# A four-layer-pair f32 transformer block on one core: narrow TensorE products gathered or widened, latent matrices folded, more weight and gate tiles, a new order table

## The reference, cut to what matters

```
x = x + L0_xattn(ctx, ctx, ln(x))      # one head, no mask
x = x + L0_ffn(ln(x))                  # switch-head: 8 heads x 8 experts, 2 chosen, values and output
x = x + L1_xattn(ln(x), ctx, ctx)      # 16 heads of 8, causal, lengths
x = x + L1_ffn(ln(x))                  # ternary weights, gelu, norm, 512 wide
x = x + L2_xattn(ln(x), ctx)           # 2 heads of 64, q and k normalized per head, mask
x = x + L2_ffn(ln(x))                  # 8 experts of 256, 2 chosen, with biases b1 and b2
x = x + L3_xattn(ln(x), ctx, ctx)      # 16 heads of 64, a bias on the scores
x = x + L3_ffn(ln(x))                  # see below
```

```
lat    = xf @ fc1.T                          # 128 -> 64
he[e]  = relu2(lat @ w1[e].T) @ w2[e].T      # 8 experts, 64 -> 64 -> 64, relu2(t) = max(t, 0)^2
comb   = sum over the 2 chosen experts of gate[e] * he[e]
routed = comb @ fc2.T                        # 64 -> 128
shared = relu2(xf @ up.T) @ down.T           # 128 -> 512 -> 128
out    = routed + shared
```

## Time and profile before

| what | value |
|---|---|
| runs | 685.36, 688.69, 686.41 us; median 686.41 us |
| span of the profiled execution | 682.8 us (the page gives no other time of its own) |
| PE busy | 654.7 us, 96% of the span |
| DVE, ACT, POOL busy | 523.3 us (77%), 372.4 us (55%), 203.6 us (30%) |
| mean granted PE clock | 9 tenths or more in all 40 slices but one |
| moved by DMA | 113.86 MB |

### The profile page before, as it was taken

One profiled execution on the slowest core, in us unless ns is written; L12 is line 12 of the kernel. 1 busy time (PEld: TensorE's weight loads), 2 busy tenths in 40 slices (PEclk: granted clock), 3 DMA queues, 4 the chain that ended last, 5 costly groups with the idle time before them and its releaser, 6 DMA issues.

```text
span 682.8 us, 14844 instructions
## 1 busy us (share of the span) xinstructions
PE 654.7 (96%) x5566; PEld 589.5 (86%) x5566; DVE 523.3 (77%) x1433; ACT 372.4 (55%) x1261; POOL 203.6 (30%) x244
## 2 busy tenths in 40 slices
PE   6889999999999999999999999999999998899898
PEld 5779999788989999998799998987899997669776
DVE  1987587995788889895788999887588866657756
ACT  2251421356664866236655686377647653966683
POOL 0010002832331422304424242135232532533140
PEclk9999999999999999999999999999999999899999
DMA  8979969987312916885346027577026500000000
GB/s 319 395 237 306 401 233 314 330 291 244 129 62 69 329 33 219 271 298 204 102 150 228 2 66 221 188 234 234 33 55 232 201 16 5 1 1 1 1 1 13
DMA packets 37655, 113.86 MB, mean 167 GB/s; under 512 B 9040, under 2 KB 11728, under 8 KB 37200
## 3 DMA queue, kind: packets, MB, share of 16 engines
q1 hardware_dynamic: 37584, 112.92, 47.9%
HBM read 111.86 MB, written 1.05 MB: 165 GB/s over the span
## 4 chain that ended last, share of the span: by engine, by line
PE 78%; DVE 12%; ACT 6%; DMA 2%; issue 1%; POOL 1%; DVEq 0%
PE bank L462 35%; PE e_bank L462 31%; PE p_bank L462 5%; PE bank L713 3%; ACT wide_b L1136 3%; DVE gated L1442 2%; DVE wide_b L1445 1%; DMA gated<-gates_of 1%; POOL wide_b L1346 1%; DVE max_neg L1728 1%; PE bank L702 1%; DVE f_route L1442 1%; ACT f_b L1045 1%; PE p_bank L562 1%; ACT wide_a L995 1%
## 5 line engine op out<-in xcount | busy, mean ns | idle before, releaser
L462 PE MATMUL e_bank<-weights,gated 128*128 128x128 f32 x2048 | 246.9, 277 | 0.3 <-ACT f_v L995 0.2
L462 PEld LDWEIGHTS e_bank<-weights,gated 128*128 128x128 f32 x2048 | 236.6, 192 | 8.2 <-issue 4.0
L1346 POOL TENSOR_TENSOR wide_b<-wide_b,row_inv 128x480 f32<-128x480 f32 x64 | 76.0, 1196 | 132.5 <-DVE row_inv L1733 132.4
L1136 ACT ACTIVATE wide_b<-wide_b,max_neg 128x120 f32<-128x120 f32 x272 | 103.5, 386 | 19.0 <-DVE max_neg L1728 16.3
L995 ACT ACTIVATE wide_a<-bank 120x512 f32<-120x512 f32 (+4 forms) x110 | 59.0, 545 | 50.9 <-PE bank L713 23.3
L1442 DVE TENSOR_TENSOR gated<-gated,f_xnT 128x1024 f32<-128x1024 f32 x64 | 81.9, 1302 | 6.3 <-DMA gated<-gates_of 5.8
L1442 DVE TENSOR_TENSOR gated<-gated,f_v 128x1024 f32<-128x1024 f32 x64 | 78.8, 1250 | 8.5 <-ACT f_v L995 4.2
L1338 POOL TENSOR_TENSOR rstd<-var_eps,w_const 128x1 f32<-128x1 f32 (+1 forms) x48 | 34.4, 717 | 144.6 <-DVE var_eps L1438 144.5
L1136 ACT ACTIVATION_READ_ACCUMULATOR wide_b<-wide_b,max_neg 128x1 f32 x272 | 52.3, 192 | 0.0
L713 PE MATMUL bank<-w_const,wide_b 128*120 128x128 f32 x256 | 40.4, 284 | 3.8 <-POOL wide_b L1346 3.7
L1728 DVE TENSOR_REDUCE max_neg<-wide_b 128x4 f32<-128x480 f32 x64 | 41.8, 653 | 2.2
(11 more groups left out here) (265 smaller groups left out, 1229.7 us busy)
## 6 DMA issues: line engine op xcount, KB each, us to landing
gated<-gates_of SPq DMA_DIRECT2D x128, 512.0 KB, 5.8
weights<-in_experts SPq DMA_DIRECT2D x64, 512.0 KB, 6.4
w_L2f<-in_L2f SPq DMA_DIRECT2D x1, 2124.0 KB, 14.6
w_L3x<-in_L3x SPq DMA_DIRECT2D x1, 2108.0 KB, 18.6
wide_b<-in_raw0f SPq DMA_DIRECT2D x1, 1024.0 KB, 7.9
w_L3f<-in_L3f SPq DMA_DIRECT2D x1, 1000.0 KB, 21.1
w_L1f<-in_L1f SPq DMA_DIRECT2D x1, 516.0 KB, 10.9
x_next<-in_x SPq DMA_DIRECT2D x4, 128.0 KB, 6.4
```

Source lines behind the costliest of these rows:

```text
L462: return nc.tensor.matmul(o, lhsT, rhs, start=first, stop=last)
L1136: last = nc.scalar.activation(p, p, ACT.Exp, bias=max_neg[lane][:, h:h + 1], accum_out=row_sum[lane][:, h:h + 1])
L1346: nc.gpsimd.tensor_tensor(p3, p3, row_inv[lane][:, 4 * i:4 * i + 4].unsqueeze(2).broadcast_to([128, 4, K]), ALU.mult).then_inc(probs_norme ...
```

## The change

1. `W_SLOTS` 4 to 6 and `G_SLOTS` 6 to 7. Four weight tiles stay where they were in the first loads; two more are loaded after the last weight pack, with a semaphore of their own.
2. The fourth L1 score product contracts all 128 rows: POOL makes a second block tensor in which all rows but the last 32 are zero.
3. The L1 mix and the L3 mix are one visit of 16 products each, after all four transposes. The L1 mix uses four groups of columns in turn.
4. The L2X scores are one product of K=128 and 240 columns; ACT makes the two heads' keys as two copies, each scaled by a column that is zero in the other head's rows. PE's wait for layer 3's keys moves behind the scores.
5. L2F: the gate sits in 128 columns, zero beyond the first 8; its transpose and the b2 product are whole.
6. L3F: at setup fc1 is multiplied into w1 and fc2 into w2, so the routed part is 128 -> 512 -> 128 like the shared one. DVE spreads the gate over 512 columns, PE transposes that in four pieces, DVE multiplies the squared hidden values by it, and four products add onto the shared sum in the same bank. w2's pack doubles from 256 to 512 columns.
7. The residual's identity product is gone; DVE adds `x_now` where it copied.
8. The table `ORDER` is new for all five engines. Its strings are not shown; of the first one a line:

```diff
-W_SLOTS, G_SLOTS = 4, 6
+W_SLOTS, EARLY_SLOTS, G_SLOTS = 6, 4, 7
...
-    "PE": "pppp0p0pp00pp0pppp0pp00pp0pppp0pffpffpfpfffpfffpf0pffffpfpfpfpfpffffpfffffpffffpfffpp0p101p0pfffpf1f0f"
...
+    "PE": "pppppp0000ppp0ppppp0000pppppppffpffpfffpfpffffpffffpfpfpfpfpffpfffffpffffpffpfffpp00p01p0ff1ffp01p0f"
...
     # SP, first loads
-                    for j in range(W_SLOTS):
-                        sp.dma_start(weights[j][:, :], experts[:, E * D * j:E * D * (j + 1)]).then_inc(first_experts, 16)
+                    first_weights(range(EARLY_SLOTS), first_experts)
...
+                    first_weights(range(EARLY_SLOTS, W_SLOTS), next_experts)
...
     # PE, front
-                                mm(e_bank[:, 0:2 * D], ident, f_x[pair % 2][:, :], True, False)
...
     # PE, setup
-                    mm(bank[1][0][:, 64:128], centre, part["L3f", "fc1"]).then_inc(centre_products, 1)
+                    mm(bank[1][0][0:64, 128:256], part["L3f", "fc1"], centre).then_inc(centre_products, 1)
+                    yield
+                    pe.wait_ge(centred, GATE_FC1)
+                    mm(bank[0][1][:, :], centred_fc1[0:64, :], part["L3f", "w1"][0:64, :]).then_inc(centre_products, 1)
+                    for p in range(4):
+                        last = mm(bank[1][1][:, 128 * p:128 * p + 128], part["L3f", "w2"][0:64, 128 * p:128 * p + 128],
+                                  part["L3f", "fc2"][0:64, :])
+                    last.then_inc(centre_products, 1)
...
     # PE, L1 scores and mix
-                    mm(bank[lane][0][:, 0:4 * K], small[lane][96:128, 0:S], wide_a[lane][96:128, 0:4 * K])\
+                    pe.wait_ge(blocks_ready[lane], blocks_ready.upto(L1X, 2, pair))
+                    mm(bank[lane][0][:, 0:4 * K], small[lane][:, 0:S], wide_a[lane][:, 512:512 + 4 * K])\
...
+                    for i in range(4):
+                        transpose_probs(L1X, i, lane)
+                        yield
+                    pe.wait_ge(blocks_ready[lane], blocks_ready.upto(L1X, 3, pair))
+                    pe.wait_ge(pT_ready[lane], pT_ready.upto(L1X, 4, pair))
+                    for c in range(4):
+                        for j in range(4):
+                            h = 4 * j + c
+                            last = mm(bank[lane][2][32 * j:32 * j + 32, 0:S], v[lane][0:K, 32 * h:32 * h + 32],
+                                      wide_a[lane][0:K, 128 * h:128 * h + 128], c == 0, c == 3)
+                    last.then_inc(mix_psum[lane], 1)
...
     # PE, L2X scores
-                    for h in range(H2X):
-                        r = slice(64 * h, 64 * h + 64)
-                        last = mm(bank[lane][2 * h][:, 0:K], wide_a[lane][r, 0:S], wide_a[lane][r, 1408:1408 + K])
-                    last.then_inc(scores_psum[lane], 1)
+                    mm(bank[lane][0][:, 0:2 * K], wide_a[lane][:, 0:S], wide_a[lane][:, 1408:1408 + 2 * K])\
+                        .then_inc(scores_psum[lane], 1)
...
     # PE, L2F
-                    mm(bank[lane][0][:, 0:D], gateT[lane][0:E, :], part["L2f", "b2"][0:E, :])\
+                    mm(bank[lane][0][:, 0:D], gateT[lane][:, :], part["L2f", "b2"])\
...
     # PE, L3F
+                    for to, name in ((0, "up"), (1, "w1")):
+                        for c in range(4):
+                            last = mm(bank[lane][to][:, 128 * c:128 * c + 128],
+                                      part["L3f", name][:, 128 * c:128 * c + 128], xnT[lane][:, :])
+                        last.then_inc(hidden_psum[lane], 1)
+                        yield
...
+                    pe.wait_ge(spread_ready[lane], spread_ready.upto(L3F, 1, pair))
                     for p in range(4):
...
+                        last = nc.tensor.transpose(bank[lane][2][:, 128 * p:128 * p + 128],
+                                                   spread[lane][:, 128 * p:128 * p + 128], ident)
+                    last.then_inc(turned_psum[lane], 1)
+                    yield
+                    pe.wait_ge(routed_gated[lane], routed_gated.upto(L3F, 1, pair))
                     for p in range(4):
...
+                        last = mm(bank[lane][0][:, 0:D], wide_a[lane][:, 512 + 128 * p:640 + 128 * p],
+                                  part["L3f", "w2"][:, 128 * p:128 * p + 128], False, p == 3)
+                    last.then_inc(out_psum[lane], 1)
...
     # DVE, L3F
-                    for odd in range(2):
-                        last = tt(wide_b[lane][:, 1024 + 256 * odd:1280 + 256 * odd].rearrange("p (c u) -> p c u", u=64),
...
-                    nc.vector.tensor_reduce(comb[lane],
...
+                    ts(spread[lane].rearrange("p (e i) -> p e i", i=64), r[6].unsqueeze(2).broadcast_to([128, E, 64]),
+                       one[2], None, ALU.mult).then_inc(spread_ready[lane], 1)
+                    yield
...
+                    tt(wide_a[lane][:, 512:1024], wide_a[lane][:, 512:1024], bank[lane][2][:, :], ALU.mult)\
+                        .then_inc(routed_gated[lane], 1)
```

More of the change, by code:

```diff
@@ L247, in build @@
         q2_turned = below[:, 0:D]
+        centred_fc1 = below[:, D:2 * D]
         p_products = Course("p_products", [
@@ L954, in back_lane @@
-                    yield
-                    pe.wait_ge(hidden_ready[lane], hidden_ready.upto(L3F, 1, pair))
-                    pe.wait_ge(gate_exp[lane], gate_exp.upto(L3F, 1, pair))
-                    for p in range(4):
-                        last = mm(bank[lane][2][:, 128 * p:128 * p + 128],
-                                  part["L3f", "w1"][0:64, 128 * p:128 * p + 128], small[lane][0:64, 0:S])
-                    last.then_inc(hidden_psum[lane], 1)
-                    yield
-                    pe.wait_ge(hidden_ready[lane], hidden_ready.upto(L3F, 3, pair))
```

200 lines of the change are left out of this document (84 added, 116 removed).

## The result

The changed kernel takes 692.36 us where the kernel before, run beside it, takes 684.44: a ratio of 1.0108, with a 95% interval of 1.0089 to 1.0127. The forecast was 660.5 us with a range of 650 to 675. The time is outside the range and the sign is wrong.

What follows compares the result with a forecast made beforehand. PE's instructions, one after the other, were taken to bound the middle. Terms -23.2 - 5.5 - 1.7 + 2.0 + 1 + 1.5 = -25.9 took the span from 682.8 to 656.9; plus 3.6 gave 660.5 us, range 650 to 675.

Steps and rivals of the forecast that it cites:

- the sum: All predicted gains and costs added up: -25.9 us over the whole span, -21.0 us in the middle.
- the terms: PE work changes: 31.0 us saved on pieces over eight lane-pairs, 1.7 on the residual, 2.0 added by setup folding.
- my two bounds: Gathered L1 mix visit: 1.00 + 0.20 us with four column groups at once, 2.00 + 0.20 with two at a time.
- rival 1: L1 mix: four column groups don't run at once, saving 0.20 instead of 1.20; 8.0 us less gain, 668.5 us; chance 0.11.
- rival 3: PE's narrow visits: the 0.20 us isn't a price of changing form; 13.4 us less gain, 674 us; chance 0.06.
- the forecast 5.5: Last stage, the last pair's back alone: 5.5 us shorter, bounds 2 and 13.
- The step on waits: Middle: PE meets a late DVE more often as DVE's share rises from 82% to 86%; +1.5 us (0 to 12).
- Rival 2: Middle becomes bound by order and DVE; half of 24.5 us saved turns into waiting, 671 us; chance 0.12.
- the sign of rival 2 or 5: Middle: PE busy falls to 96% instead of above 98.5%, with waits on DVE or ACT's copies ahead of the mixes.
- Rival 5: PE's queue stands at 16 gathered mixes awaiting the fourth copy; up to 708 us; chance 0.05, plus 0.02 for breaking even.
- The 3.6 us: Distance from the old profiled span, 682.8 us, to the runs' median, 686.41, added to the predicted span of 656.9.

Runs made afterwards that it cites:

- the second table: The changed kernel's code with a third order table, searched from the first re-made one with corrected durations: 663.72 us, 0.9692 of the kernel before.

## Why the prediction was wrong

**What held.** The reading that PE bounds the middle, and most of the prices. That the middle of the second table fits the sum within about 1 us is partly the luck of the cut. Over the whole span, where no cut matters, PE's busy time fell there by 27.7 us (654.7 to 626.9), against 30.7 by the terms (31.0 + 1.7 - 2.0). Some of the 27.7 is the clock: PE is busy for 13.6 us at the lower level in the kernel before (from 36.6, 582.7 and 647.6 us on) and for 4.6 in the second table (from 35.3), which makes some 4.5 us. So 23 to 28 of the 30.7 came, and of the 21.0 us by which the second table beats the kernel before, 4 to 5 are a gain that the sum did not have.

The gathered mix takes the lower of my two bounds, 1.01 us; rival 1 falls. So does rival 3: the wide records beside a narrow visit still take longer, 1.89 us for 16 behind one visit, and wide ones between wide neighbours still take 1.78 (155.71 to 157.49 in the changed kernel). The Trainium skill (TensorE: Matmul & The Clock Gate, "Measured speedup vs the span model") has 2.38 times for three column groups; here 32 records take 1.01 us on four groups where 32 whole ones take 3.56, a factor of 3.5, which no row of before showed.

The tail's 6.0 us for the forecast 5.5 was luck in good part. The kernel before has some 10 us of PE work at the lower clock in its tail and the changed one 3.4 (from 664.7 us), a difference worth about 3.4 us by the same estimate; and in the second table, with more work behind the cut and the clock at 1.00, the tail gained 3.0.

**What failed.** The step on waits: "PE's idle time in the middle is 4.2 us; I add a third, +1.5 (0 to 12, see the rivals)". It was worked out from DVE's share of busy time, as if waits grew with an engine's load. DVE's share in fact fell, from 82% to 78%, and its late tiles are not on top of the list. What matters is where each instruction stands in five fixed lists. The changed table differs in every line, and I took its quality for that of the old one. Measured: 21.1 us more waiting in the middle than before, and about 7 us of low clock beside it, for which the sum had no term at all. The two edits on which waits on loads or on POOL could be blamed were moved or taken out, one at a time, and the loss stayed; with another table, all else equal, the loss is gone. The wait for the first blocks is traced to its place in the lists; the many smaller waits behind it are put down to the order as a whole, since whole tables were exchanged there.

**What could have been seen.** The order of the instructions was open before the run: POOL's masks of both lanes ahead of the first block, behind a folding step that had moved from inside the first front to its end. I looked at three places where the edits move instructions, and not at the place where the first backs begin, where the table alone moves them. A sum over removed work needs, for each engine's first use of a stage, the question what it stands behind.

**The rivals.** Rival 2 had the right direction, half of the gain turned into waiting, with 671 us; what came was more than all of it: PE was busy for 94.5% of the middle, where the prediction had named 96% as the sign of rival 2 or 5. Rival 5 had the right sign at the wrong place: PE's queue hardly stands at the gathered mixes (one wait of 0.5 us on an ACT copy there), but at POOL's products in front of transposes and scores. Together they had 0.17, and the sign a chance of 0.05. A table made anew for five engines deserved a chance of its own of being the worse one and a price from the order itself: POOL's first block came at 143.72 us here and at 131.33 in the second table, and here PE stood 5.3 us for it, with 3 to 4 us of low clock behind.

**The start.** I took +1 for 1.18 MB more of loads. The loads cost nothing that could be measured, and the table cost 3 us.

**The base.** The 3.6 us that I added between the profiled span and the median belonged to two different executions. Wherever a run has both figures on record they stand 1.3 to 2.6 us apart, mostly 1.3 or 1.4. This put the forecast some 2 us too high and had no part in the wrong sign.

## What to carry to other kernels

When a change rewrites a fixed order together with the work in it, price the two apart: the work by starts in the trace, the order by building the code in two orders. A bound engine at 99% is as much a property of the order as of the work, and an order is fitted to one code: put under other instructions, it lost 3% here. If PE must pause, look at the clock behind the pause too: behind one of 5.3 us it cost another 3 to 4 here.

## What the runs showed of the hardware

**A pause can cost twice.** From a pause of 5.27 us on PE's granted clock was at the lower level, 1.2 GHz, until 152.7 us; 40 idle transposes in the pause kept it at 2.4 GHz there, and the work up to the first L1 mix took 2.8 us less. Pauses of 1.5 and 2.0 us were each followed by a shorter stretch at the lower level in the changed kernel. The 32 records of an L3 mix, 1.89 us elsewhere in the same kernel (256.44 to 258.33), took 3.5 there:

```profile
290.98 0.62 PE L728 MATMUL bank<-w_const,wide_b 128*120 128x128 f32 x4 [1.50 <-POOL wide_b L1334]
...
292.54 3.58 PE L469 MATMUL bank<-wide_a,v 120*64 120x128 f32 x32
```

But not every such pause is followed by one. The same wait of 2.0 us stands in the kernel with the filled pause, and there the clock stays at 1.00 behind it (PE's timeline, then the columns of the stages); what tells the two apart, no row shows.

```profile
171.61 0.62 PE L728 MATMUL bank<-w_const,wide_b 128*120 128x128 f32 x4 [2.03 <-POOL wide_b L1337]
```

```profile
172.10:177.40 5.30, 5.30 (x45) 4.76 (x44) 4.40 (x15) 4.46 (x22) 1.90 (x3) 1.00 0.17 53
```

**DVE and POOL hold each other up.** In the changed kernel DVE's scaling of 64 columns, 0.38 us on average over 16, takes 1.62 us for two when POOL has just begun a 512-column product, and POOL's next normalization, one of 64 with a mean of 1.16 us, takes 1.88 beside DVE's gated product. The first fence is DVE's timeline, the second POOL's:

```profile
170.69 1.62 DVE L1433 TENSOR_SCALAR small<-wide_a,mean_var,rstd 120x64 f32<-120x64 f32 x2 [1.03 <-POOL rstd L1392]
...
173.56 1.20 DVE L1436 TENSOR_TENSOR gated<-gated,f_xnT 128x1024 f32<-128x1024 f32 x1
```

```profile
170.62 1.27 POOL L1376 TENSOR_TENSOR v<-small,w_const 120x512 f32<-120x512 f32 x1
...
173.72 1.88 POOL L1334 TENSOR_TENSOR wide_b<-wide_b,row_inv 128x480 f32<-128x480 f32 x1 [1.47 <-DVE row_inv L1729]
```

PE's next transposes, at 175.75, wait 2.02 us for that last product. The Trainium skill (SBUF — State Buffer, "SBUF: two separate sides") says that the two engines share a pair of ports, and that between a POOL instruction and one of DVE that needs the pair (in a two-port mode, or with two inputs in SBUF while POOL reads SBUF) whichever starts first keeps it for its whole instruction. The rows agree: DVE's two scalings end 0.4 us behind POOL's product, which began 0.07 us ahead of them, and POOL's normalization ends 0.8 us behind the gated product, which began 0.16 us ahead of it. No run here separates the two engines, and no row shows which mode DVE's scaling runs in.
